# Cross attention to 257 keys: the last key in one product, the heads picked out by VectorE, the row sums split between ScalarE and VectorE

## The chip, the cores and the metric

The kernel runs on one core of a Trainium2 chip. Its time is the device time of the whole program, in microseconds (us). TensorE is PE in the rows (PEld is its weight load), VectorE is DVE, ScalarE is ACT, GpSimd is POOL and SyncE is SP.

## The reference, cut to what matters

The program is a stack of twelve sublayers on x of 128 x 32 tokens with 128 channels. Sublayers 1, 7 and 10 are cross attentions of 16 heads (8 channels each) to a context of 257 keys for each batch row; the change is in these alone. The first reads:

```python
scale = HEAD_DIM ** (-0.5)
q = (xq @ Wq.T).reshape(B, SQ, NUM_HEADS, HEAD_DIM)
kv = (xkv @ Wkv.T).reshape(B, SKV, 2, NUM_HEADS, HEAD_DIM)
k, v = (kv[:, :, 0], kv[:, :, 1])
att = jax.nn.softmax(jnp.einsum('bxhd,byhd->bhxy', q, k) * scale, axis=-1)
x = jnp.einsum('bhxy,byhd->bxhd', att, v).reshape(B, SQ, H)
return x @ Wout.T + bout
```

The tenth also masks keys: `scores = jnp.where(mask == 0, -1e9, scores)`. All data are float32.

## The kernel before

`cross_attention` runs three times, under the names a_cross, e_cross and t_cross (the one with the mask). Each engine has its own program, written by hand; semaphores tie them together, and every engine works strictly in the order in which its program is written. The 128 batch rows are 32 tiles of four (4 x 32 tokens = 128 partitions). A batch row is a step `step(i, n)`; the loop body holds eight steps, so two tiles. A head has 8 channels; four heads make a group of 32 channels (G = 4 groups, J = 4 places in a group).

For batch row n, PE computes the scores of the four groups into PSUM banks 0 to 3 (`scores`, L2071; with a mask another product each, L2076). `scores(n + 1)` waits for all exponentials of n. DVE takes the negative maxima (`maximum`, L2250), ACT the exponentials E (L2214), DVE their sums and reciprocals (L2260, L2262), POOL multiplies E by the reciprocals (`unit`, L2013), PE turns E (L2125, the first half into bank T_BANK, the second into K_BANK), DVE and ACT copy the halves to ET (L2256, L2199), and PE multiplies with the values (`values`, L2135) into O_BANK. The key projection of the next row (L2055) also uses K_BANK and so waits for ACT's copy of ET; ACT then copies the keys (L2193), just ahead of the next exponentials. In a step PE's order is: scores(n), project_keys(n + 1), side(n), project_values(n + 1), both turns of n - 2, values of n - 3. ACT's is: side_out, second half of ET of n - 3, keys of n + 1, exponentials of n, values of n + 1.

257 keys are two blocks of 128 and one key. Once per tile the last key is added apart. Its weights lie in E's last column; PE turns that column for four batch rows and four groups (L2096, 16 rows), ACT copies it (E_last, L2186). Its values come from a product with the context's last columns, four times repeated (L2111, 16 rows), ACT copies them (v_raw, L2189) and POOL spreads them by `last16` (L2017). Four products (L2144, `last_key`, after the values in the third step of the next tile) add them into O_BANK. O_BANK holds for every channel the results of all four heads of its group; only one of four is its own. ACT copies the bank whole (L2207), and the output projection is four products (L2104) with `wo_of`, a weight that is zero but for one head place each. DVE adds the result to X (L2270).

## Time and profile before

| | us |
|---|---|
| median of 3 runs | 4606.94 |
| lowest and highest | 4599.29, 4607.55 |
| profiled execution | 4604.74 |
| its span | 4602.9 |

The span is from the first to the last instruction of the profiled execution. Busy times are those of one engine; several engines are busy at once, and idle time of one that nobody waits for costs nothing. PEclk is the TensorE clock that was granted, as a share of full speed.

### The profile page before, as it was taken

To read this page: it belongs to the slowest core of one execution; us is meant where nothing else is said; L and a number is where in the kernel's file an instruction comes from. 1 tells how busy PE (TensorE), PEld (TensorE's weight loads), DVE (VectorE), ACT (ScalarE), POOL (GpSimd) and SP (SyncE) were. 2 spreads that over 40 slices of the span, in tenths; PEclk is the share of its full clock that TensorE was granted. 3 is DMA by queue.
4 is the path that set the end of the run, shared out by engine and by line. 5 is a ranking of instruction groups with operands and counts; after the bars stand their busy time and mean duration, and the time that the engine had idled before them with its cause. 6 is when DMAs were issued, how large, how long until landed. Compare 5 with 4: busy or idle time off the path is not lost. (4 is left out here: it accounts for less than half of the span.)

```text
span 4602.9 us, 120099 instructions
## 1 busy us (share of the span) xinstructions
PE 3609.7 (78%) x45714; PEld 2581.9 (56%) x45718; DVE 2836.1 (62%) x6649; ACT 2347.0 (51%) x5169; POOL 2397.8 (52%) x2417
## 2 busy tenths in 40 slices
PE   6999959999998288792966999975389998666836
PEld 4777746666665166452644777643267776343424
DVE  6877756666565424674346778735767776743635
ACT  4777635555554043570214777732367775534613
POOL 5666556666664434663344666642246654714623
PEclk9999979999999599895987999975589999877958
DMA  1111010000000122101221111000010111000023
GB/s 59 33 33 33 24 61 9 5 7 10 10 2 2 58 76 65 35 4 64 73 60 32 35 34 33 24 7 6 0 39 31 33 33 51 2 1 5 2 74 88
DMA packets 90228, 143.73 MB, mean 31 GB/s; under 512 B 9984, under 2 KB 66432, under 8 KB 89344
## 3 DMA queue, kind: packets, MB, share of 16 engines
q1 hardware_dynamic: 79616, 117.56, 8.0%
q0 software_dynamic: 10240, 20.99, 1.6%
q8 instruction: 261, 4.28, 0.4%
q14 instruction: 111, 0.91, 0.1%
HBM read 107.44 MB, written 31.06 MB: 30 GB/s over the span
## 5 line engine op out<-in xcount | busy, mean ns | idle before, releaser
L2013 POOL TENSOR_TENSOR t_cross_E<-t_cross_E,t_cross_inverse 128x1028 f32<-128x1028 f32 x128 | 243.4, 1901 | 218.3 <-DVE t_cross_inverse L2262 218.3
L2013 POOL TENSOR_TENSOR e_cross_E<-e_cross_E,e_cross_inverse 128x1028 f32<-128x1028 f32 x128 | 243.4, 1901 | 207.4 <-DVE e_cross_inverse L2262 207.4
L2013 POOL TENSOR_TENSOR a_cross_E<-a_cross_E,a_cross_inverse 128x1028 f32<-128x1028 f32 x128 | 243.4, 1901 | 205.3 <-DVE a_cross_inverse L2262 205.3
L2810 PE MATMUL l_psum<-l_ffn_w,l_hidden 128*128 128x128 f32 x1536 | 218.4, 285 | 32.4 <-POOL l_hidden L2684 30.8
L2250 DVE TENSOR_REDUCE t_cross_negtop<-t_cross_psum 128x2 f32<-128x514 f32 x256 | 165.4, 688 | 119.7 <-PE t_cross_psum L2076 119.7
L2250 DVE TENSOR_REDUCE e_cross_negtop<-e_cross_psum 128x2 f32<-128x514 f32 x256 | 165.4, 688 | 106.9 <-PE e_cross_psum L2071 105.7
L2810 PEld LDWEIGHTS l_psum<-l_ffn_w,l_hidden 128*128 128x128 f32 x1536 | 190.6, 192 | 70.5 <-POOL l_hidden L2684 42.0
L2250 DVE TENSOR_REDUCE a_cross_negtop<-a_cross_psum 128x2 f32<-128x514 f32 x256 | 165.4, 688 | 105.1 <-PE a_cross_psum L2071 103.7
L2803 PE MATMUL l_psum<-l_hT,l_ffn_w 128*128 128x512 f32 x384 | 204.4, 635 | 0.9 <-ACT l_hT L2867 0.9
L2214 ACT ACTIVATE a_cross_E<-a_cross_psum,a_cross_negtop 128x257 f32<-128x257 f32 x512 | 200.5, 481 | 0.6 <-DVE a_cross_negtop L2250 0.6
L2214 ACT ACTIVATE t_cross_E<-t_cross_psum,t_cross_negtop 128x257 f32<-128x257 f32 x512 | 200.5, 481 | 0.7 <-DVE t_cross_negtop L2250 0.7
L2214 ACT ACTIVATE e_cross_E<-e_cross_psum,e_cross_negtop 128x257 f32<-128x257 f32 x512 | 200.5, 481 | 0.6 <-DVE e_cross_negtop L2250 0.6
L2684 POOL TENSOR_TENSOR l_hidden<-l_hidden,l_less 128x512 f32<-128x512 f32 x96 | 120.1, 1274 | 94.7 <-ACT l_hidden L2891 94.7
L2663 POOL TENSOR_SCALAR l_normed<-inner,l_moments,l_rstd 128x128 f32<-128x128 f32 x192 | 159.1, 840 | 15.1 <-POOL l_rstd L2657 15.1
L2964 DVE TENSOR_TENSOR inner<-l_psum,inner 128x512 f32<-128x512 f32 x48 | 33.2, 691 | 213.4 <-PE l_psum L2795 213.4
L2260 DVE TENSOR_REDUCE t_cross_total<-t_cross_E 128x4 f32<-128x1028 f32 x128 | 155.4, 1214 | 0.0
L2260 DVE TENSOR_REDUCE a_cross_total<-a_cross_E 128x4 f32<-128x1028 f32 x128 | 155.3, 1214 | 0.0
L2260 DVE TENSOR_REDUCE e_cross_total<-e_cross_E 128x4 f32<-128x1028 f32 x128 | 155.3, 1213 | 0.0
L2674 POOL TENSOR_TENSOR l_q<-l_q,l_q_stat 128x512 f32<-128x512 f32 x48 | 50.8, 1059 | 185.4 <-DVE l_q_stat L2944 185.4
L2125 PE MATMUL t_cross_psum<-const_sb,t_cross_E 128*128 128x128 f32 x1024 | 135.5, 276 | 2.9 <-POOL t_cross_E L2013 2.9
L2125 PE MATMUL e_cross_psum<-const_sb,e_cross_E 128*128 128x128 f32 x1024 | 134.2, 274 | 2.9 <-POOL e_cross_E L2013 2.9
L2125 PE MATMUL a_cross_psum<-const_sb,a_cross_E 128*128 128x128 f32 x1024 | 133.9, 274 | 2.9 <-POOL a_cross_E L2013 2.9
(747 smaller groups left out, 11209.8 us busy)
## 6 DMA issues: line engine op xcount, KB each, us to landing
a_cross_context<-context SPq DMA_DIRECT2D x32, 522.0 KB, 3.3
e_cross_context<-context SPq DMA_DIRECT2D x32, 522.0 KB, 3.3
t_cross_context<-context SPq DMA_DIRECT2D x32, 522.0 KB, 3.3
u_moe_all_weights<-pack_u_moe SPq DMA_DIRECT2D x1, 5633.0 KB, 16.4
slots<-l_blank SPq DMA_DIRECT2D x6, 832.0 KB, 12.7
a_moe_x_slots<-slots SPq DMA_DIRECT2D x26, 192.0 KB, 2.9
slots<-a_moe_y_slots SPq DMA_DIRECT2D x26, 192.0 KB, 2.1
c_moe_x_slots<-slots SPq DMA_DIRECT2D x26, 192.0 KB, 2.7
```

Source lines behind the costliest of these rows:

```text
L2013: pool.tensor_tensor(E[:, n % N], E[:, n % N], spread(inverse[:, n % 4], SK, 2), ALU.mult).then_inc(s_unit, 1)
L2125: last = pe.transpose(psum[:, (T_BANK, K_BANK)[c], g * P:(g + 1) * P], E[:, n % N, g, c * P:(c + 1) * P], ident)
L2214: act.activation(E[:, n % N, g], psum[:, g, 0:SK], ACT.Exp, bias=negtop[:, n % 2, g:g + 1]).then_inc(s_exp, 1)
L2250: dve.tensor_reduce(negtop[:, n % 2, at], psum[:, at, 0:SK], AX.X, ALU.max, negate=True).then_inc(s_top, 1)
L2260: dve.tensor_reduce(total[:, n % 2], E[:, n % N], AX.X, ALU.add).then_inc(s_sum, 1)
L2663: last = pool.tensor_scalar(Y1[:, t], c.tile(t), moments[:, 0, t, 0:1], rstd[:, 0, 1, t:t + 1], ALU.subtract, ALU.mult)
L2674: pool.tensor_tensor(groups, groups, spread(q_stat[:, 2], DH, 2), ALU.mult).then_inc(s_soft, 1)
L2684: pool.tensor_tensor(hidden[:, f], hidden[:, f], less[:, f - 2], ALU.add).then_inc(s_late, 1)
L2803: pe.matmul(psum[:, U_BANKS[f % 2]], c.ffn(f * P), hT2[:], start=True, stop=True).then_inc(s_up, 1)
L2810: last = pe.matmul(psum[:, D_BANK, t * P:(t + 1) * P], hidden[:, f, t * P:(t + 1) * P], c.ffn((NF + f) * P), start=(f == 0 and t == 0), st ...
L2964: dve.tensor_tensor(c.chunk(), tiles(psum[:, C_BANK]), c.chunk(), ALU.add).then_inc(s_mid, 1)
```

## The change

The last key's four products become one, and the output projection's four become one.

- **Last key.** POOL makes `last_of`: E's last column of four batch rows and four groups, four times over, times a constant that keeps for each place its own 32 partitions. One small product with `fold` (64 rows, 32 columns) gives for each of 64 pairs (batch row, head) the weights of 32 queries; DVE multiplies them by `own_batch` into E_last. The last key's values are computed in 64 rows (the context's last columns now 16 times repeated), and DVE multiplies them by `own_head` into v_last. One product of v_last and E_last gives the last key's part of the output, apart from O_BANK. ACT copies it to aT.
- **Heads picked out.** DVE adds to aT, for each of the four places j, the bank O_BANK times a column that is 1 for the channels whose head is at place j (L2286 of the changed kernel, four times, each waiting for the one before). Two stand ahead of the maxima and two behind them. Then one product with wo.
- **Sums.** Two of four exponentials also write their sum along the row (`accum_out`); DVE sums the other two groups only.

```diff
+    c["own_place"] = (row[:, None] // S == np.arange(4)[None]).astype(float)
+    c["own_batch"] = (row[:, None] // 16 == np.arange(BPT)[None]).astype(float)
+    c["own_head"] = (row[:, None] % 16 == ch[None] // 8).astype(float)
...
+    SUMMED = 2
-    LAST = BPT * G
+    LAST = BPT * G * J
...
-            def last_values(i, t):
-                pool.wait_ge(s_raw, i * 2 + t + 1)
-                pool.tensor_tensor(v_last[:, t % 2], spread(v_raw[:, t % 2], BPT, 1),
-                                   core.const("last16")[0:LAST].rearrange("p (b c) -> p b c", c=P), ALU.mult).then_inc(s_last, 1)
+            def last_weights(i, t):
+                h = t % 2 * BPT
+                pool.wait_ge(s_unit, i * N + 4 * t + 4)
+                if tile_exists(i, t - 2):
+                    pool.wait_ge(s_el, i * 2 + t - 1)
+                pool.tensor_tensor(last_of[:, t % 2], spread(E[:, h:h + BPT, :, MAIN], J, 3),
+                                   spread(spread(core.const("own_place"), G, 1), BPT, 1), ALU.mult).then_inc(s_last_of, 1)
...
                 if n % 4 == 1:
...
-                        pe.transpose(psum[0:LAST, V_BANK, SIDE], E[:, h:h + 4, :, MAIN].rearrange("p n g -> p (n g)"),
-                                     ident).then_inc(s_el, 1)
+                        pe.wait_ge(s_last_of, i * 2 + t)
+                        pe.matmul(psum[0:LAST, V_BANK, 2 * P:2 * P + S], last_of[:, (t - 1) % 2].rearrange("p b g j -> p (b g j)"),
+                                  core.const("fold"), start=True, stop=True).then_inc(s_el, 1)
+                    if tile_exists(i, t - 2):
+                        pe.wait_ge(s_aT, i * 2 + t - 1)
+                        pe.matmul(psum[:, V_BANK, BESIDE], aT[:, t % 2], w("wo"), start=True, stop=True).then_inc(s_out, 1)
                 if n % 4 == 2:
+                    if tile_exists(i, t - 2):
+                        pe.wait_ge(s_done, i * 2 + t - 1)
...
-                        pe.wait_ge(s_O, i * 2 + t - 1)
-                        for j in range(J):
-                            last = pe.matmul(psum[:, V_BANK, SIDE], O[:, t % 2, j].rearrange("p b s -> p (b s)"), wo_of[:, j],
-                                             start=(j == 0), stop=(j == J - 1))
+                        pe.matmul(psum[:, V_BANK, SIDE], v_last[:, (t - 1) % 2], E_last[:].rearrange("p b s -> p (b s)"),
+                                  start=True, stop=True).then_inc(s_alone, 1)
...
                 if n % 4 == 0 and tile_exists(i, n // 4 - 1):
-                    pe.wait_ge(s_O, i * 2 + n // 4)
+                    pe.wait_ge(s_aT, i * 2 + n // 4)
...
-                for b in range(BPT):
-                    last = pe.matmul(psum[:, O_BANK, b * P:(b + 1) * P], v_last[:, t % 2, b], E_last[:, t % 2],
-                                     start=False, stop=(b == BPT - 1))
...
-                    act.activation(E_last[:, (t - 1) % 2], psum[0:LAST, V_BANK, SIDE], ACT.Copy).then_inc(s_E_last, 1)
-                    act.activation(v_raw[:, t % 2], psum[0:LAST, V_BANK, SIDE], ACT.Copy).then_inc(s_raw, 1)
+                if n % 4 == 2 and tile_exists(i, t - 1):
+                    act.wait_ge(s_alone, i * 2 + t)
+                    if tile_exists(i, t - 3):
+                        act.wait_ge(s_out, i * 2 + t - 2)
+                    act.activation(aT[:, (t - 1) % 2], psum[:, V_BANK, SIDE], ACT.Copy).then_inc(s_begun, 1)
...
-                act.activation(O[:, t % 2].rearrange("p j b s -> p b j s"),
-                               psum[:, O_BANK].rearrange("p (b j s) -> p b j s", b=BPT, s=S), ACT.Copy).then_inc(s_O, 1)
...
+                    if g < SUMMED:
+                        act.activation(E[:, n % N, g], psum[:, g, 0:SK], ACT.Exp, bias=negtop[:, n % 2, g:g + 1],
+                                       accum_out=total[:, n % 2, g:g + 1]).then_inc(s_exp, 1)
...
-                dve.tensor_reduce(total[:, n % 2], E[:, n % N], AX.X, ALU.add).then_inc(s_sum, 1)
+                dve.tensor_reduce(total[:, n % 2, SUMMED:], E[:, n % N, SUMMED:], AX.X, ALU.add).then_inc(s_sum, 1)
...
+            def pick(i, t, places):
+                out = aT[:, t % 2].rearrange("p (b s) -> p b s", s=S)
+                for j in places:
+                    if j == 0:
+                        dve.wait_ge(s_begun, i * 2 + t + 1)
+                        dve.wait_ge(s_pv, i * N + 4 * t + 4)
+                    else:
+                        dve.wait_ge(s_picked, (i * 2 + t) * 3 + j)
+                    dve.scalar_tensor_tensor(out=out, in0=psum[:, O_BANK].rearrange("p (b j s) -> p b j s", b=BPT, s=S)[:, :, j],
+                                             scalar=in_group[:, j:j + 1], in1=out, op0=ALU.mult, op1=ALU.add
+                                             ).then_inc(s_aT if j == J - 1 else s_picked, 1)
...
-                              np.repeat(context[:, :, SK - 1].reshape(P, TILES, BPT), 4, axis=2)], axis=2)
+                              np.repeat(context[:, :, SK - 1].reshape(P, TILES, BPT), 16, axis=2)], axis=2)
```

The order of instructions is written by hand. PE's queue in the third step of a tile, from the scores to those of the fourth, stood so before (names are output<-inputs, then output rows x columns; L2055 projects keys, L2059 values, L2125 turns E):

```order
L2071 MATMUL a_cross_psum<-a_cross_kT,a_cross_q_heads 128x257 x4
L2055 MATMUL a_cross_psum<-a_cross_context,a_cross_weights 128x257
L2104 MATMUL a_cross_psum<-a_cross_wo_of,a_cross_O 128x128 x4
L2059 MATMUL a_cross_psum<-a_cross_weights,a_cross_context 128x128 x2
L2125 MATMUL a_cross_psum<-const_sb,a_cross_E 128x128 x4
L2121 REGISTER_ALU
L2125 MATMUL a_cross_psum<-const_sb,a_cross_E 128x128 x4
L2135 MATMUL a_cross_psum<-a_cross_ET,a_cross_v 32x128 x8
L2144 MATMUL a_cross_psum<-a_cross_E_last,a_cross_v_last 128x128 x4
L2068 REGISTER_ALU
L2071 MATMUL a_cross_psum<-a_cross_kT,a_cross_q_heads 128x257 x4
```

and stands so now (L2077 are the scores, L2061 and L2065 the projections, L2131 the turns, L2141 the values):

```order
L2077 MATMUL a_cross_psum<-a_cross_kT,a_cross_q_heads 128x257 x4
L2061 MATMUL a_cross_psum<-a_cross_context,a_cross_weights 128x257
L2111 MATMUL a_cross_psum<-a_cross_E_last,a_cross_v_last 128x128
L2065 MATMUL a_cross_psum<-a_cross_weights,a_cross_context 128x128 x2
L2131 MATMUL a_cross_psum<-const_sb,a_cross_E 128x128 x4
L2127 REGISTER_ALU
L2131 MATMUL a_cross_psum<-const_sb,a_cross_E 128x128 x4
L2141 MATMUL a_cross_psum<-a_cross_ET,a_cross_v 32x128 x8
L2074 REGISTER_ALU
L2077 MATMUL a_cross_psum<-a_cross_kT,a_cross_q_heads 128x257 x4
```

The four products with wo_of have become the one with v_last, and nothing stands between the values and the next scores.

DVE's queue before, in the eighth step (the fourth of the second tile), from the third step's copy of ET on; total is the sum, inverse its reciprocal, negtop the maxima:

```order
L2256 COPY a_cross_ET<-a_cross_psum 128x512
L2250 TENSOR_REDUCE a_cross_negtop<-a_cross_psum 128x2 x2
L2260 TENSOR_REDUCE a_cross_total<-a_cross_E 128x4
L2262 RECIPROCAL a_cross_inverse<-a_cross_total 128x4
L2256 COPY a_cross_ET<-a_cross_psum 128x512
```

and now:

```order
L2247 COPY a_cross_ET<-a_cross_psum 128x512
L2286 SCALAR_TENSOR_TENSOR a_cross_aT<-a_cross_psum,const_sb,a_cross_aT 128x128 x2
L2241 TENSOR_REDUCE a_cross_negtop<-a_cross_psum 128x2 x2
L2286 SCALAR_TENSOR_TENSOR a_cross_aT<-a_cross_psum,const_sb,a_cross_aT 128x128 x2
L2251 TENSOR_REDUCE a_cross_total<-a_cross_E 128x2
L2253 RECIPROCAL a_cross_inverse<-a_cross_total 128x4
L2247 COPY a_cross_ET<-a_cross_psum 128x512
L2274 TENSOR_TENSOR a_cross_v_last<-a_cross_psum,const_sb 64x128
```

Two picks into aT stand ahead of the maxima (negtop), two between them and the sums (total), and the multiplication that makes v_last closes the step.

## Rows read from the trace of the kernel before

**Rows 1.** The page, busy time of each engine over the whole span.
```profile
PE 3609.7 (78%) x45714; PEld 2581.9 (56%) x45718; DVE 2836.1 (62%) x6649; ACT 2347.0 (51%) x5169; POOL 2397.8 (52%) x2417
```

**Rows 2.** Windows: stretch, us; busy PE, PEld, DVE, ACT, POOL; PEclk; DMA share; GB/s.
```profile
303.00:319.32 16.32, 15.51 (x174) 11.59 (x173) 13.04 (x22) 11.89 (x33) 10.07 (x7) 1.00 0.10 33
...
3619.00:3635.65 16.65, 16.00 (x193) 12.16 (x193) 12.97 (x22) 11.88 (x33) 10.00 (x8) 1.00 0.10 32
...
1800.00:1820.00 20.00, 16.83 (x95) 12.21 (x94) 7.22 (x21) 7.06 (x14) 2.92 (x4) 1.00 0.15 40
```

**Rows 3.** Timeline of ACT: start, duration, engine, line, out<-in, count; exponentials at tile starts.
```profile
303.11 1.56 ACT L2214 ACTIVATE a_cross_E<-a_cross_psum,a_cross_negtop 128x257 f32<-128x257 f32 x4
...
314.56 1.57 ACT L2214 ACTIVATE a_cross_E<-a_cross_psum,a_cross_negtop 128x257 f32<-128x257 f32 x4
...
319.49 1.57 ACT L2214 ACTIVATE a_cross_E<-a_cross_psum,a_cross_negtop 128x257 f32<-128x257 f32 x4
...
335.75 1.56 ACT L2214 ACTIVATE a_cross_E<-a_cross_psum,a_cross_negtop 128x257 f32<-128x257 f32 x4
...
3616.93 1.57 ACT L2214 ACTIVATE t_cross_E<-t_cross_psum,t_cross_negtop 128x257 f32<-128x257 f32 x4
...
3650.22 1.56 ACT L2214 ACTIVATE t_cross_E<-t_cross_psum,t_cross_negtop 128x257 f32<-128x257 f32 x4
```

**Rows 4.** Timeline, one ordinary step of a_cross on ACT and PE, and ET's copy later.
```profile
306.92 1.56 ACT L2214 ACTIVATE a_cross_E<-a_cross_psum,a_cross_negtop 128x257 f32<-128x257 f32 x4
...
308.35 0.41 ACT L2203 ACTIVATE a_cross_v<-a_cross_psum 128x256 f32<-128x256 f32 x1
...
308.62 0.40 ACT L2177 ACTIVATE a_cross_qT<-a_cross_psum,a_cross_bq 128x128 f32<-128x128 f32 x1
...
308.87 0.64 ACT L2199 ACTIVATE a_cross_ET<-a_cross_psum 128x512 f32<-128x512 f32 x1
...
309.65 0.67 PE L2055 MATMUL a_cross_psum<-a_cross_context,a_cross_weights 128*128 128x257 f32 x2 [0.38 <-ACT a_cross_ET L2199]
...
310.73 1.57 ACT L2214 ACTIVATE a_cross_E<-a_cross_psum,a_cross_negtop 128x257 f32<-128x257 f32 x4
...
316.39 0.60 ACT L2199 ACTIVATE a_cross_ET<-a_cross_psum 128x512 f32<-128x512 f32 x1
```

**Rows 5.** Timeline of PE in the third and fourth steps of the same tile.
```profile
313.98 1.05 PE L2104 MATMUL a_cross_psum<-a_cross_wo_of,a_cross_O 128*128 128x128 f32 x8
...
314.87 0.61 PE L2059 MATMUL a_cross_psum<-a_cross_weights,a_cross_context 128*128 128x128 f32 x4
...
316.86 1.04 PE L2144 MATMUL a_cross_psum<-a_cross_E_last,a_cross_v_last 16*128 16x128 f32 x7
...
317.64 0.49 PE L2071 MATMUL a_cross_psum<-a_cross_kT,a_cross_q_heads 32*128 32x257 f32 x3
...
318.38 0.70 PE L2055 MATMUL a_cross_psum<-a_cross_context,a_cross_weights 128*128 128x257 f32 x2
...
319.01 0.39 PE L2111 MATMUL a_cross_psum<-a_cross_weights,a_cross_context 128*16 128x128 f32 x2
```

**Rows 6.** Groups by line in a_cross: count, busy us, mean ns, idle time before.
```profile
L2250 DVE TENSOR_REDUCE a_cross_negtop<-a_cross_psum 128x2 f32<-128x514 f32 x256 | 165.4, 688 | 105.1 <-PE a_cross_psum L2071 103.7
L2260 DVE TENSOR_REDUCE a_cross_total<-a_cross_E 128x4 f32<-128x1028 f32 x128 | 155.3, 1214 | 0.0
...
L2022 POOL TENSOR_TENSOR X<-X,a_cross_bo 128x128 f32 x28 | 12.7, 454 | 0.0
...
L2189 ACT ACTIVATE a_cross_v_raw<-a_cross_psum 16x128 f32<-16x128 f32 x32 | 8.0, 250 | 0.0
```

**Rows 7.** Single lines elsewhere: count, duration ns min/median/max, first and last start, form.
```profile
L1516 ACT ACTIVATE a_moe_r<-a_moe_ex x1: 229/229/229, 1578.7 to 1578.7; 128x32 f32<-128x32 f32 x1
...
L1712 DVE SCALAR_TENSOR_TENSOR X<-a_moe_got,a_moe_part,X x64: 342/346/403, 1737.3 to 1860.1; 128x128 f32<-128x128 f32 x64
```

**Rows 8.** Timeline, the first instruction of DVE.
```profile
13.90 0.49 DVE L208 BATCH_NORM_STATS2 a_cross_front_ln_stats<-X 128x6 f32<-128x128 f32 x2 [13.90 <-PEq L3026]
```

More of the change, by code:

```diff
@@ L1960, in cross_attention @@
         s_t0, s_t1, s_ET0, s_ET1, s_pv = sc.sem("t0"), sc.sem("t1"), sc.sem("ET0"), sc.sem("ET1"), sc.sem("pv")
-        s_vl, s_raw, s_last = sc.sem("vl"), sc.sem("raw"), sc.sem("last")
-        s_el, s_E_last, s_whole, s_O = sc.sem("el"), sc.sem("E_last"), sc.sem("whole"), sc.sem("O")
+        s_vl, s_v_last, s_last_of = sc.sem("vl"), sc.sem("v_last"), sc.sem("last_of")
+        s_el, s_E_last, s_alone, s_begun = sc.sem("el"), sc.sem("E_last"), sc.sem("alone"), sc.sem("begun")
+        s_picked, s_aT = sc.sem("picked"), sc.sem("aT")
         s_out, s_base, s_done = sc.sem("out"), sc.sem("base"), sc.sem("done")
@@ L2219, in step @@
                     second_half(i, n - 3)
-                if n % 4 == 3 and tile_exists(i, n // 4 - 1):
-                    whole(i, n // 4 - 1)
                 if exists(i, n + 1):
```

72 lines of the change are left out of this document (36 added, 36 removed).

## The prediction, made before the changed kernel had run

> **What bounds the kernel now.** I read the page first, then the timeline of one tile inside a cross attention, then the groups of costliest instructions. The page says that TensorE (PE) is busy for 78% of the span [rows 1], but that is an average over twelve sublayers, and the change touches only the three cross attentions. There the profile of one tile shows PE busy for 15.51 of 16.32 us at full clock, VectorE (DVE) for 13.04, ScalarE (ACT) for 11.89 and GpSimd (POOL) for 10.07; in t_cross, which adds a mask product, 16.00 of 16.65 [rows 2]. Two consecutive tiles give the periods: from the exponentials at 303.11 to those at 335.75 are two tiles, 16.32 us each; in t_cross (3650.22 - 3616.93) / 2 = 16.65 [rows 3].
>
> A tile is four steps, one for each batch row. The starts of the exponentials are 303.11, 306.92, 310.73, 314.56 and 319.49 [rows 3, 4]: three steps of 3.81 to 3.83 us and one of 4.93. The ordinary step is a ring between ACT and PE, to be read in one step [rows 4]: exponentials from 306.92, copy of the values at 308.35 (+1.43), copy of the queries at 308.62 (+0.27), copy of the turned weights ET at 308.87 (+0.25) that ends at 309.51 (+0.64), key projection on PE at 309.65 (+0.14, it waited for that copy), next exponentials at 310.73 (+1.08: the projection's 0.67, a signal, and the key copy). The sum is 3.81. Without the queries' copy, and with the 0.60 that the ET copy takes elsewhere (316.39), the ring is 3.81 - 0.25 - 0.04 = 3.52. The long step is another thing: ACT's ET copy ended at 316.39 + 0.60 = 316.99, so the key projection could start at 317.13, and it starts at 318.38, 1.25 us later [rows 4, 5]. PE had stood in its own queue: output projection (L2104) 313.98 to the next product at 314.87 is 0.89, and the last key's products (L2144) 316.86 to the scores at 317.64 are 0.78 [rows 5]. So the tile is three rings and one stretch of pure PE queue.
>
> **The change, part by part.** *PE loses* the four products of L2144 (0.78) and three of the four of L2104: 0.89 falls to a quarter, 0.22 [rows 5]. *It gains* one product of the last key (v_last by E_last): 0.22 for a plain one, 0.39 as L2111's row has for a single one with weights of another shape [rows 5]; I take 0.32. It also gains a small product with 64 columns in place of the transposition of 16 (+0.1, half of a plain product, since it moves 32 columns but twice). PE's queue would fall from 16.32 to 16.32 - 0.78 - 0.89 + 0.22 + 0.32 + 0.1 + 0.1 = 15.4; the last 0.1 is an estimate for one more switch of weight shapes, from the excess of 0.32 over 0.22.
>
> *ACT loses* E_last and v_raw (0.25 each [rows 6]) and the copy "whole". Neighbours overlap: the queries' row is 0.40 and the next one starts 0.25 later [rows 4]; with 0.09 to 0.15 of overlap a row of 0.25 costs the ring 0.10 to 0.16. ACT gains the copy that begins aT, 128 x 128 without a pointer: 0.16 too, since a row of 16 x 128 has as many elements to a partition. It stands in the ring of the fourth step.
>
> *The ring then sets the end.* With PE out of the way the tile is four rings, 4 x 3.52, plus queries 0.25 + 0.04, plus aT 0.16: 14.53; I take 14.5. Into every ring the change puts a new term: two of the four exponentials also write their sum (L2205). Call r what one such sum adds to the ring; the tile is then **14.5 + 8 r**. No row of the trace has an accumulator output, so r is bounded by the nearest rows. Lower end: an ACT instruction that overlaps its neighbours costs 0.16 for 128 elements and 0.27 for 256 (308.35 to 308.62), so one element leaves 0.16 - 0.11 = 0.05, say 0.06 [rows 4, 6]. Upper end: the read has to await the end of its exponential, which gives up the overlap (spacing 1.43 / 4 = 0.36, one row 1.56 - 3 x 0.36 = 0.48 [rows 4], so 0.12), and then takes a whole small row, 0.20 to 0.23 after L1516's 229 ns for 32 elements [rows 6, 7]: 0.32 to 0.35. I take the middle, **r = 0.19**: I expect the lost overlap, or a good part of it, and a small instruction that itself overlaps. The tile is then 14.5 + 1.52 = 16.02, against 16.32: -0.30. For t_cross the scores need the mask product too; the same tile plus 0.08 for that, 16.10 against 16.65: -0.55.
> The Trainium skill, "VectorE: DVE Perf Modes", section "Two Vector instructions with no wait between them", says that an operation that also writes out its accumulator is two instructions, the main one and an accumulator read. It says so of VectorE; if ScalarE does likewise, each of the 768 summed exponentials here brings a second instruction, and the rule speaks against the change; no row of this trace can show it.
>
> *DVE* reduces two heads' groups instead of four: 1.21 falls to about 0.69, which L2250 takes for 514 elements [rows 6]. Per tile that is -4 x 0.52 = -2.1. It gains E_last and v_last and four picks of 128 x 128 with a pointer, 0.35 each at most (L1712 [rows 7]), the picks 0.40 apart because each waits for the one before: +2.1. DVE's busy time stays at 13.0, so its load does not matter; its order does. Two picks stand ahead of the maxima of the fourth step, and the next exponentials wait behind them. From the start of the last exponential: 0.36 + values copy 0.26 + aT 0.31 + 0.05 + picks 0.80 + first maximum 0.69 + 0.04 = 2.51. The ring's own way there is 0.36 + 0.26 + 0.16 + 0.60 + 0.14 + 1.08 = 2.60. They are covered by 0.09 us, no more. The last two picks delay sums, reciprocal and POOL's product, but what waits for that (the turn two steps on) comes after the scores of the following step, and the shorter sum gives back 0.52 of the 0.80. The new wait of PE's values on aT is for something 1.5 us old.
>
> *POOL* loses the 512 elements of L2017 and gains a product of 64 elements, between nothing and 0.45 (the row of L2022 has 128 elements and 0.45 [rows 6]). PE now waits for it before the small product of the second step, where it already waited for POOL's unit(); that step has the longest ring, so some 0.3 more is covered.
>
> *Outside the loop.* The constants shrink from 1943 to 1567 columns; with X's 4096 the first instruction that needs them starts at 13.90 [rows 8], so at most 376 / 6039 x 13.9 = -0.9 us; I take 0.8. The context's load grows by 48 of 1044 columns and the transfers are a tenth of the window. PE's busy share falls to about 14.4 / 16.0 = 90%; a stretch with 16.83 of 20 busy was granted full clock [rows 2], so I charge nothing.
>
> **The sum.** The first tiles and the last have no or only part of this; I count 29 of 32. 2 x 29 x 0.30 = 17.4, 29 x 0.55 = 16.0, 0.8 at the start: -34 us. The profiled execution took 4604.7 (span 4602.9), the median is 4606.9; 4604.7 - 34 = 4571, on the median's scale **4573 us**.
>
> **The rivals.** *B, the sums cost more than they free (slower).* The accumulator read waits and blocks, r = 0.28: the tile is 14.5 + 2.24 = 16.74 everywhere, +0.42 in a and e, +0.09 in t: 58 x 0.42 + 29 x 0.09 - 0.8 = +26, 4633. At r = 0.32 it would be 4662. It decides from r = 0.24, where 58 x (8r - 1.82) + 29 x (8r - 2.15) = 0. For it: the ring has no slack of its own; against: small ACT rows do overlap. The skill's rule, taken for ScalarE, is this case with two full small instructions.
> *C, the sums are nearly free.* At r = 0.06 the ring is 15.0, and PE's own queue of 15.4 to 15.6 takes over: -0.8 and -1.0 a tile, 58 x 0.8 + 29 x 1.0 + 0.8 = -76; at r = 0.11 the ring and queue mix, about -56. I put the case at 4542.
> *D, the picks come late.* If the picks are 0.50 apart and not 0.40, the fourth step's exponentials wait 0.11 more and the late reciprocals another 0.15: 0.3 a tile eats the gain, 87 x 0.3 = 26, 4599. For it: the cover is 0.09.
> *E, the stall does not go.* If something else stood behind PE's queue in the long step, that step would stay at 4.93 and the other three would grow by 2 r each: 87 x 1.14 = +99, 4706. Against: the ET copy was done 1.39 us before the projection [rows 4, 5].
>
> **How the numbers follow.** Forecast (r from 0.13 to 0.225) 0.43; C 0.17; D 0.13; B 0.25; E 0.02. Faster by over 0.2% (9 us, about what a measurement of this kernel can tell from no change) is the forecast, C and a third of D: 0.64. Within it is the rest of D and a little of B: 0.11. Slower: 0.25. The range goes from 4545 (near C's point) to 4633 (B's point); beyond them lie some 0.2.
>
> **What would show it.** Right: the period of the exponentials near 16.0 with no long step; the two summed exponentials spaced 0.55 instead of 0.36; no PE wait over 0.4 ahead of the key projection that ACT did not cause. Wrong: the spacing of the summed ones at 0.64 or more (B) or under 0.45 (C); maxima that end after the key copy in the fourth step (D); the long step still there (E).

## The result, and the profile after

| | before | after |
|---|---|---|
| median of 4 runs each, us | 4603.11 | 4529.06 |
| lowest and highest, us | 4597.06, 4607.55 | 4522.06, 4535.61 |
| span of the profiled execution, us | 4602.9 | 4529.1 |

The ratio is 0.984, with a 95% interval from 0.9819 to 0.986: 74 us or 1.6% faster. In a second comparison on another occasion (e0 below) it was 0.987, from 0.9842 to 0.9898, or 60 us; one of the four executions there took 4624.59 us at a lower granted clock (0.824 against 0.891 to 0.894) and is not in that ratio. When the forecast was made the median before was 4606.94, of three executions; with a fourth it is 4603.11. The forecast was 4573, 34 us under the former, with a range from 4545: the direction was right, the gain more than twice as large, and the time outside the range.

Below, "interval" means the time from the first exponential of one step to that of the next; a tile has four. The queries are copied in the **first**, the small product of the last key stands in the **second**, the long one of before and the copy that begins aT are the **third**. Means are over 24 tiles of a_cross, from the starts of the exponentials in the trace.

| interval, us | first | second | third | fourth | tile | tile in t_cross |
|---|---|---|---|---|---|---|
| before | 3.81 | 3.82 | 4.94 | 3.75 | 16.32 | 16.65 |
| after | 4.00 | 4.01 | 3.90 | 3.80 | 15.71 | 15.90 |

The page after, busy time of each engine (against [rows 1]): PE and DVE fell by 75 and 26 us; ACT's rows went from 5169 to 5745.
```profile
PE 3535.1 (78%) x44662; PEld 2466.6 (54%) x44662; DVE 2810.2 (62%) x7222; ACT 2348.1 (52%) x5745; POOL 2329.9 (51%) x2417
```

Windows after, one tile of a_cross and one of t_cross (against [rows 2]; columns as there):
```profile
302.04:317.75 15.71, 15.00 (x164) 10.61 (x164) 12.85 (x28) 12.01 (x40) 9.35 (x7) 1.00 0.11 36
3570.00:3585.90 15.90, 15.40 (x181) 11.06 (x180) 12.79 (x29) 12.03 (x41) 9.34 (x7) 1.00 0.11 35
```
The clock is full in both, as before. PE is still busy for 95% of a tile of a_cross, and yet this says little: the first and the third interval are set by something else, as a table further down shows.

Timeline after, from the end of the first interval to the start of the fourth (against [rows 4, 5]):
```profile
301.32 0.32 POOL L2023 TENSOR_TENSOR a_cross_last_of<-a_cross_E,const_sb 128x64 f32<-128x64 f32 x1 [0.18 <-POOL a_cross_E L2015]
...
301.79 0.27 PE L2101 MATMUL a_cross_psum<-const_sb,a_cross_last_of 128*64 128x32 f32 x2 [0.16 <-POOL a_cross_last_of L2023]
...
302.04 0.47 ACT L2205 ACTIVATE a_cross_E<-a_cross_psum,a_cross_negtop 128x257 f32<-128x257 f32 x1
...
302.40 0.20 ACT L2205 ACTIVATION_READ_ACCUMULATOR a_cross_E<-a_cross_psum,a_cross_negtop 128x1 f32 x1
302.49 0.48 ACT L2205 ACTIVATE a_cross_E<-a_cross_psum,a_cross_negtop 128x257 f32<-128x257 f32 x1
...
302.94 0.85 ACT L2208 ACTIVATE a_cross_E<-a_cross_psum,a_cross_negtop 128x257 f32<-128x257 f32 x2
...
303.92 0.63 ACT L2194 ACTIVATE a_cross_ET<-a_cross_psum 128x512 f32<-128x512 f32 x1
...
304.95 0.70 PE L2061 MATMUL a_cross_psum<-a_cross_context,a_cross_weights 128*128 128x257 f32 x2
...
306.06 0.47 ACT L2205 ACTIVATE a_cross_E<-a_cross_psum,a_cross_negtop 128x257 f32<-128x257 f32 x1
...
308.10 0.64 ACT L2194 ACTIVATE a_cross_ET<-a_cross_psum 128x512 f32<-128x512 f32 x1
...
308.29 0.74 DVE L2286 SCALAR_TENSOR_TENSOR a_cross_aT<-a_cross_psum,const_sb,a_cross_aT 128x128 f32<-128x128 f32 x2 [0.42 <-ACT a_cross_aT L2184]
...
308.88 0.67 PE L2061 MATMUL a_cross_psum<-a_cross_context,a_cross_weights 128*128 128x257 f32 x2
...
308.94 1.28 DVE L2241 TENSOR_REDUCE a_cross_negtop<-a_cross_psum 128x2 f32<-128x514 f32 x2
...
309.96 0.47 ACT L2205 ACTIVATE a_cross_E<-a_cross_psum,a_cross_negtop 128x257 f32<-128x257 f32 x1
```
Three things are to be seen. A sum on ScalarE is a second row, ACTIVATION_READ_ACCUMULATOR, 0.20 us long; it starts 0.36 us after its exponential, where the next exponential would have started, and the next one starts at +0.45 (302.04, 302.49, 302.94). A sum therefore adds **0.09 us**. PE's small product (L2101) waits 0.16 us for POOL's product of 64 elements. And the long interval is gone: 306.06 to 309.96 is 3.90. PE had waited at this place before too, in the second step, for POOL's unit(). Timeline of before:
```profile
310.70 0.27 PE L2096 MATMUL a_cross_psum<-const_sb,a_cross_E 128*16 128x128 f32 x1 [0.38 <-POOL a_cross_E L2013]
```

Over the whole program, from the first instruction that computes with a sublayer's weights to its last, a_cross lost 19.6 us, e_cross 21.4 and t_cross 23.8, together 64.8 of the 73.8 us between the two spans. The other 9 lie in code that the change does not touch: the stretch between e_cross and t_cross took 342.6 us before and 329.8 after, and that between a_cross and e_cross 1884.3 before and 1888.4 after. Windows of before and then of after, the first stretch behind e_cross:
```profile
3000.46:3143.09 142.63, 115.02 (x2966) 67.01 (x2967) 60.57 (x156) 53.95 (x88) 65.54 (x92) 0.79 0.02 7
```
```profile
2963.40:3106.00 142.60, 110.06 (x3332) 66.97 (x3332) 64.68 (x166) 57.35 (x92) 67.80 (x94) 0.87 0.02 7
```
After does more matrix products in the same time (3332 against 2966), at a granted clock of 0.87 against 0.79. In the traces of all kernels below this stretch between the sublayers was either 329 to 332 us, with a clock of 0.85 to 0.88 in its first 142.6 us, or 336 to 343, with 0.79 to 0.83. It did not go with the speed: 340.9 us in the fastest (e7), 342.8 in e11, 328.9 in e0, 329.2 in e13. It may go with the sums: all six kernels with no sum on ScalarE had the long one, and nine of the twelve with some had the short one. With one trace of each kernel what decides it stays open, and so does whether these 13 us belong to the change. The intervals are the better measure of the mechanism.

### The profile page after: what moved, and what is told of

Its sections match the earlier page's. It is cut to its first block and busy times, and to the rows that moved or that the text cites. A ratio compares the mean times of both kernels' runs of the same rounds, so it can differ in the third digit from the quotient of the medians.

```text
span 4529.1 us, 119692 instructions
## 1 busy us (share of the span) xinstructions
PE 3535.1 (78%) x44662; PEld 2466.6 (54%) x44662; DVE 2810.2 (62%) x7222; ACT 2348.1 (52%) x5745; POOL 2329.9 (51%) x2417
## 5 line engine op out<-in xcount | busy, mean ns | idle before, releaser
L2131 PE MATMUL a_cross_psum<-const_sb,a_cross_E 128*128 128x128 f32 x1024 | 134.6, 275 | 2.2 <-POOL a_cross_E L2015 2.1
L2131 PE MATMUL e_cross_psum<-const_sb,e_cross_E 128*128 128x128 f32 x1024 | 134.4, 275 | 2.2 <-POOL e_cross_E L2015 2.1
L2131 PE MATMUL t_cross_psum<-const_sb,t_cross_E 128*128 128x128 f32 x1024 | 134.3, 275 | 2.1 <-POOL t_cross_E L2015 2.1
L2814 PEld LDWEIGHTS l_psum<-l_qT,l_ctx 32*32 32x32 f32 x6144 | 65.7, 107 | 115.8 <-issue 110.1
L2188 ACT ACTIVATE t_cross_kT<-t_cross_psum,t_cross_weights 128x257 f32<-128x257 f32 x128 | 61.0, 477 | 129.1 <-PE t_cross_psum L2061 129.1
L2188 ACT ACTIVATE a_cross_kT<-a_cross_psum,a_cross_weights 128x257 f32<-128x257 f32 x128 | 61.0, 477 | 121.2 <-PE a_cross_psum L2061 121.2
L2188 ACT ACTIVATE e_cross_kT<-e_cross_psum,e_cross_weights 128x257 f32<-128x257 f32 x128 | 61.0, 477 | 120.1 <-PE e_cross_psum L2061 120.1
L2205 ACT ACTIVATE e_cross_E<-e_cross_psum,e_cross_negtop 128x257 f32<-128x257 f32 x256 | 118.6, 473 | 0.9 <-DVE e_cross_negtop L2241 0.9
L2205 ACT ACTIVATE a_cross_E<-a_cross_psum,a_cross_negtop 128x257 f32<-128x257 f32 x256 | 118.6, 473 | 0.9 <-DVE a_cross_negtop L2241 0.9
```

The source lines that it names most:

```text
L2131: last = pe.transpose(psum[:, (T_BANK, K_BANK)[c], g * P:(g + 1) * P], E[:, n % N, g, c * P:(c + 1) * P], ident)
L2188: act.activation(kT[:, n % 2], psum[:, K_BANK, 0:SK], ACT.Identity, bias=w("bk")).then_inc(s_k, 1)
L2205: act.activation(E[:, n % N, g], psum[:, g, 0:SK], ACT.Exp, bias=negtop[:, n % 2, g:g + 1], accum_out=total[:, n % 2, g:g + 1]).then_inc(s ...
L2814: last = pe.matmul(psum[rows, C_BANK, b * S:(b + 1) * S], ctx[rows, b], qT[rows, b * S:(b + 1) * S], start=True, stop=True)
```

## The experiments

All ratios are to the kernel before, run beside it on the same chip; "us" is what they make of some 4595. Intervals as above, from a_cross. e7 leaves out three quarters of two kinds of products, and e14 and e15 take the last key's weights from another tile, so these three do not compute the whole result.

| run | ratio (95%) | us | first | second | third | fourth | tile |
|---|---|---|---|---|---|---|---|
| e0, changed kernel again | 0.987 (0.9842 to 0.9898) | -60 | 4.00 | 4.01 | 3.90 | 3.81 | 15.72 |
| e1, no sum on ACT | 1.0004 (0.9991 to 1.0017) | +2 | 3.94 | 4.82 | 3.78 | 3.82 | 16.36 |
| e3b, one | 0.9914 (0.9888 to 0.9939) | -40 | 3.91 | 4.37 | 3.82 | 3.79 | 15.89 |
| e3, three | 0.988 (0.9859 to 0.9901) | -55 | 4.08 | 3.82 | 3.99 | 3.85 | 15.74 |
| e2, four | 0.9922 (0.9901 to 0.9942) | -36 | 4.17 | 3.91 | 4.08 | 3.90 | 16.06 |
| e4, before + split | 1.0056 (1.0038 to 1.0075) | +26 | 3.99 | 3.83 | 4.93 | 3.82 | 16.57 |
| e7, before, short products | 0.9712 (0.9691 to 0.9732) | -132 | 3.81 | 3.83 | 3.59 | 3.76 | 14.98 |
| e15, e1 without the wait | 0.9807 (0.9779 to 0.9835) | -89 | 3.94 | 3.82 | 3.78 | 3.82 | 15.36 |
| e14, changed, no wait | 0.9819 (0.9796 to 0.9841) | -83 | 3.99 | 3.82 | 3.90 | 3.80 | 15.51 |
| e8, picks behind | 0.9967 (0.9957 to 0.9978) | -15 | 3.99 | 4.02 | 3.90 | 4.18 | 16.09 |
| e9, products behind | 0.9985 (0.9973 to 0.9997) | -7 | 4.00 | 4.52 | 3.91 | 3.81 | 16.22 |
| e10, e9 with one sum | 0.9935 (0.9916 to 0.9953) | -30 | 3.90 | 4.42 | 3.81 | 3.80 | 15.93 |
| e11, e9 with none | 0.9923 (0.9906 to 0.9941) | -35 | 3.93 | 4.33 | 3.78 | 3.83 | 15.87 |
| e12, later | 0.9807 (0.9787 to 0.9827) | -89 | 4.00 | 3.78 | 3.86 | 3.82 | 15.46 |
| e13, later, one sum | 0.9793 (0.9774 to 0.9813) | -95 | 3.90 | 3.78 | 3.82 | 3.80 | 15.30 |
| e16, later, none | 0.9842 (0.9817 to 0.9867) | -73 | 3.97 | 3.78 | 3.92 | 3.97 | 15.64 |

One more reading of the traces tells what sets an interval. On ScalarE the next exponentials stand behind the copy of the keys, this waits for PE's key projection, and that for ScalarE's copy of ET. In the ring of the prediction the key projection starts 0.14 us after the copy of ET ends. Where it starts later, PE was still busy with its own queue or had been held up in it. The time from the end of the copy to the key projection, us, mean of the same 24 tiles (the fourth apart for the two tiles of a loop body):

| run | first | second | third | fourth |
|---|---|---|---|---|
| before | 0.14 | 0.29 | 1.39 | 0.15, 0.29 |
| after | 0.14 | 0.39 | 0.14 | 0.14, 0.25 |
| e14 | 0.14 | 0.21 | 0.14 | 0.14, 0.25 |
| e15 | 0.24 | 0.38 | 0.17 | 0.29, 0.42 |
| e12 | 0.14 | 0.15 | 0.19 | 0.14, 0.26 |
| e13 | 0.14 | 0.26 | 0.29 | 0.20, 0.35 |

So before the change only the first interval was the ring's, and the fourth nearly so in every other tile. Now the first and the third are (308.10 + 0.64 + 0.14 = 308.88 in the timeline above), and the fourth in every other tile, where it is 3.74; in the other it is 3.87. The second is PE's.

**The parts one by one: e7, e4.** e7 is the kernel before with

```
-                        for j in range(J):
+                        for j in range(1):
...
-                for b in range(BPT):
+                for b in range(BPT - 1, BPT):
```


> The kernel before with one product instead of four for the output projection and one instead of four for the last key; everything else stays. It leaves out three quarters of both products, so the outputs are not whole. Q: PE's queue of a tile falls by 3/4 x (0.89 + 0.78) = 1.25 us, the long step of 4.93 goes to about 3.8, the tile to 15.1 to 15.4: 87 x 1.0 = -87 us, 4516 us (4500 to 4535). S: without shorter sums on VectorE the stall only moves and the gain is a third of that or less, above 4570 us.

Measured -132 us, more than either theory: Q had the long interval go to 3.8, and counted fewer tiles. Timeline of e7, the exponentials of one tile and the output projection:
```profile
299.56 1.56 ACT L2214 ACTIVATE a_cross_E<-a_cross_psum,a_cross_negtop 128x257 f32<-128x257 f32 x4
...
303.37 1.56 ACT L2214 ACTIVATE a_cross_E<-a_cross_psum,a_cross_negtop 128x257 f32<-128x257 f32 x4
...
306.63 0.39 PE L2104 MATMUL a_cross_psum<-a_cross_wo_of,a_cross_O 128*128 128x128 f32 x2
...
307.20 1.56 ACT L2214 ACTIVATE a_cross_E<-a_cross_psum,a_cross_negtop 128x257 f32<-128x257 f32 x4
...
310.80 1.56 ACT L2214 ACTIVATE a_cross_E<-a_cross_psum,a_cross_negtop 128x257 f32<-128x257 f32 x4
```
The third interval, 307.20 to 310.80, is 3.60 where it was 4.94; the others are as before. The whole 1.34 us of a tile come from PE's queue in that one interval, and VectorE, with all its sums, is not in the way. So the changed kernel's 0.61 is 1.34 less 0.73 that the rest of the change costs.

e4 is the kernel before with `accum_out` in two exponentials and VectorE's sum over the other two.

> The kernel before with nothing but the split of the sums (two of the four exponentials write theirs, VectorE reduces the other two groups). Q: the ring of three steps grows by 0.18 each, the long step, which PE's queue sets, does not: +0.54 x 87 = +47 us at most, less what earlier reciprocals and POOL products give back; 4615 to 4650 us. S: the split is itself a good part of the gain and this kernel is faster than before, 4560 us or so.

The first interval grew by 0.18, two sums at 0.09. The long one, set by PE's queue, did not; in the second and fourth only 0.01 and 0.07 of the 0.18 came through, so those had not been rings alone, as the table above also says. By itself the split costs 26 us.

**How many sums: e1, e3b, e3, e2, e0.** The changed kernel with
```
-    SUMMED = 2
+    SUMMED = 0
```
and with 1, 3 and 4 (with 4 VectorE's sum is gone).

> The changed kernel with all four sums on VectorE again (SUMMED = 0): the products for the last key, the four picks and the order stay. Theory Q (queue): the gain is PE's queue made shorter, and a sum on ScalarE is only a cost of 0.09 us in the ring, eight of them in a tile. Then this kernel is faster than the changed one until PE's queue of about 15.4 us bounds it: 87 tiles x 0.3 = 26 us, 4503 us. Theory S (sums): the picks filled VectorE, 13.0 us a tile with the split and 15.1 without it, so without the split its sums end late, POOL's product and PE's turns follow late, and the tile goes to 16.2 or more: no better than the kernel before, 4595 to 4640 us. I lean to S here.

> The changed kernel with one sum of four on ScalarE (SUMMED = 1), between the changed kernel and e1. Each tile saves 4 x 0.09 us in the ring, in three of the four steps; VectorE's sum takes 0.26 us longer, so reciprocal, POOL's products and the small product of the second step come later. W: the second step goes from 4.01 to 4.3 us or so and the three others give back 0.27: level with the changed kernel, 65 to 80 us under the kernel before. If the sums on ScalarE were the only thing that counts: 105 us under it; if VectorE's load were: some 40 us.

> The changed kernel with three of four sums on ScalarE. The second step was 4.82, 4.37 and 4.01 us with none, one and two, and 3.91 with all four, where ScalarE's ring must set it; the three others together 11.54, 11.52, 11.70 and 12.15. With three: second step 3.8 to 3.9, the others 11.9: 15.75 a tile, level with the changed kernel, 65 to 75 us under the kernel before. My first sum, 14.5 + 4 r for each sum, would have had 0.36 more a tile: 31 us slower than the changed kernel.

> The changed kernel with all four sums on ScalarE (SUMMED = 4); VectorE makes only the reciprocal, behind the last exponential. Q with 0.09 us a sum: eight more in a tile, +0.72 less the 0.3 of the one step that PE's queue and not the ring sets: +0.4 x 87 = +36 us, 4565 us. A theory of the sums in which VectorE is still the bound would have it faster than the changed kernel: 0.69 us of each step leaves VectorE's way to the reciprocal, 87 x 0.2 or more, below 4510 us. The spacing of all exponentials should be 0.45 us.

> The changed kernel once more, beside the three that follow: 74 us under the kernel before, within 8.

With no sum on ScalarE the whole gain is gone. But it is gone in one interval: the second is 4.82, 4.37, 4.01, 3.82, 3.91 with none, one, two, three and four sums, while the first goes from 3.94 to 4.17 and the third from 3.78 to 4.08. e3b was further from the changed kernel than I expected: the second interval grew by 0.36, and the three others gave back 0.18 and not 0.27, since the fourth hardly follows the sums. Its 40 us are the number that the expectation had for VectorE's load as the cause; e15 below, with the same load as e1 and 89 us gained, rules that out. Three sums are level with two; with three or four the second interval is on the ring (0.14 from the copy to the key projection in both). Timeline of e1, the second interval:
```profile
308.80 1.90 POOL L2015 TENSOR_TENSOR a_cross_E<-a_cross_E,a_cross_inverse 128x1028 f32<-128x1028 f32 x1 [1.42 <-DVE a_cross_inverse L2253]
...
310.79 1.56 ACT L2208 ACTIVATE a_cross_E<-a_cross_psum,a_cross_negtop 128x257 f32<-128x257 f32 x4
310.88 0.32 POOL L2023 TENSOR_TENSOR a_cross_last_of<-a_cross_E,const_sb 128x64 f32<-128x64 f32 x1 [0.18 <-POOL a_cross_E L2015]
...
311.34 0.27 PE L2101 MATMUL a_cross_psum<-const_sb,a_cross_last_of 128*64 128x32 f32 x2 [0.96 <-POOL a_cross_last_of L2023]
...
315.61 1.56 ACT L2208 ACTIVATE a_cross_E<-a_cross_psum,a_cross_negtop 128x257 f32<-128x257 f32 x4
```
PE stands 0.96 us before the small product, for POOL, which waited for VectorE's reciprocal. What e1 lost to the changed kernel is this wait: VectorE's sum is part of a chain sum, reciprocal, POOL's unit(), POOL's last_weights(), PE. The record of L2101's waits says it for all of a_cross, in e1 and then after (us, times; after has the wait in the other tiles too, 0.14 us at 317.42, too short for this view):
```profile
  POOL a_cross_last_of L2023: 31.2, 33
```
```profile
  POOL a_cross_last_of L2023: 2.5, 15
```

**The wait taken away: e15, e14.** In both the small product reads the weights of the tile before, which POOL finished long ago:
```
-                        pe.wait_ge(s_last_of, i * 2 + t)
+                        pe.wait_ge(s_last_of, i * 2 + t - 1)
...
-                        pe.matmul(psum[0:LAST, V_BANK, 2 * P:2 * P + S], last_of[:, (t - 1) % 2].rearrange("p b g j -> p (b g j)"),
+                        pe.matmul(psum[0:LAST, V_BANK, 2 * P:2 * P + S], last_of[:, older % 2].rearrange("p b g j -> p (b g j)"),
```
`older` is t, that is the buffer of tile t - 2. POOL's own wait for s_el moves with it, and the first tile keeps its own weights.

> e1 (the changed kernel, no sum on ScalarE) with one thing taken away: PE's small product reads the last key's weights of the tile before, which POOL finished a tile ago, and so does not wait; the output's share of the last key is that of a wrong tile. Theory W (the wait on POOL is what made e1 slow): the second step falls from 4.82 us to about 3.9, the tile from 16.36 to about 15.4, 84 us under e1 and as much under the kernel before. Theory V (VectorE's load and the order of its sums is the bound): the time stays within 30 us of e1, which was level with the kernel before.

> The changed kernel with its two sums on ScalarE; only PE's small product reads the last key's weights of the tile before and so never waits for POOL; the output's share of the last key is that of a wrong tile. W: the second step falls from 4.01 us by the 0.16 that PE stands there, and by what the other steps' sums delay, to 3.8 or 3.85; the others stay at 4.00, 3.90, 3.80: 15.55 a tile, 13 us under the changed kernel. If the second step stays at 4.0, the length of PE's queue sets it and not the wait.

e15 is e1 with the second interval at 3.82 in place of 4.82 and nothing else moved: 1.00 us a tile, 91 us. In the changed kernel the same wait costs 4.01 - 3.82 = 0.19 us a tile; e14 is 23 us under e0 by the two ratios, 18 by the medians (4512.83 and 4530.6). And without the wait the sums on ScalarE are a loss: 15.51 with two of them, 15.36 with none. The PE rows of e15 in that interval:
```profile
310.80 0.72 PE L2077 MATMUL a_cross_psum<-a_cross_kT,a_cross_q_heads 32*128 32x257 f32 x8
311.44 0.70 PE L2061 MATMUL a_cross_psum<-a_cross_context,a_cross_weights 128*128 128x257 f32 x2
312.07 0.30 PE L2105 MATMUL a_cross_psum<-const_sb,a_cross_last_of 128*64 128x32 f32 x2
312.31 0.49 PE L2109 MATMUL a_cross_psum<-a_cross_weights,a_cross_aT 128*128 128x128 f32 x2
312.63 0.61 PE L2065 MATMUL a_cross_psum<-a_cross_weights,a_cross_context 128*128 128x128 f32 x4
...
314.62 0.71 PE L2077 MATMUL a_cross_psum<-a_cross_kT,a_cross_q_heads 32*128 32x257 f32 x8
```
No row waits; 310.80 to 314.62 is 3.82, the length of PE's own queue in this interval. It is the floor there, above the ring.

**The picks: e8.** All four picks behind the maxima of the fourth step.

> The changed kernel with all four picks behind the maxima of the fourth step, none ahead. My sum had the two picks ahead of the maxima covered by 0.09 us. If they are covered, this changes nothing or loses some us (sums, reciprocal and POOL's product of that step come 0.35 us later): 65 to 76 us under the kernel before. If they were late (rival D), the step of 3.90 us falls to the ring's 3.86 or less by more than 0.1 us, 9 us or more are gained.

The third interval, which the two picks ahead of the maxima could have delayed, stays at 3.90: they were covered. The fourth grew from 3.80 to 4.18, and the whole is 45 us behind e0, which neither expectation had. Timeline of e8:
```profile
315.15 0.47 ACT L2205 ACTIVATE a_cross_E<-a_cross_psum,a_cross_negtop 128x257 f32<-128x257 f32 x1
315.27 1.50 DVE L2286 SCALAR_TENSOR_TENSOR a_cross_aT<-a_cross_psum,const_sb,a_cross_aT 128x128 f32<-128x128 f32 x4
...
316.69 0.68 DVE L2251 TENSOR_REDUCE a_cross_total<-a_cross_E 128x2 f32<-128x514 f32 x1
...
316.92 0.64 PE L2141 MATMUL a_cross_psum<-a_cross_ET,a_cross_v 128*32 128x128 f32 x16 [0.30 <-DVE a_cross_aT L2286]
```
PE's values() of the next tile waits 0.30 for the last pick, which must have left the bank. The cover that counted was this one, behind the maxima, not that ahead of them.

**The two products moved to the end of the second step: e9, e10, e11.**
```
                 if exists(i, n - 3):
                     values(i, n - 3)
+                if n % 4 == 1:
+                    behind(i, n)
```
behind() holds the output projection and the small product, which side() gives up. It waits for s_v first, that is for ScalarE's copy of the values out of the bank to which the two write.

> The changed kernel with the last key's small product (which waits for POOL's product of 64 elements) and the output projection moved from the middle of the second step's PE work to its end, behind the values' products. Theory W (a new wait): the 0.16 us that PE stands before the small product, and the 0.3 us that the two products push the values' projection, the turns and the next key projection back, are 0.3 us of each tile; moved to the end they lie in the shadow of the exponentials and 87 x 0.3 = 26 us go: 98 to 102 us under the kernel before. Theory L (length of PE's queue): the products take the same time wherever they stand, and the time stays 74 us under the kernel before, or loses a little because VectorE gets E_last later, just ahead of the next maxima.

> As e9, but only one of four sums on ScalarE (SUMMED = 1). W: four sums at 0.09 us leave the ring of each tile, 87 x 0.36 = 31 us, and VectorE's sum, 0.26 us longer, is not waited for any more: 120 to 130 us under the kernel before. If VectorE's later sums are still waited for (by POOL's product, then the turns), it is no better than e9.

> As e9, but no sum on ScalarE (SUMMED = 0); against e1, which had these sums and the products in the middle, it tells what the wait for POOL's product was worth. W: in e1 PE stood 0.96 us before the small product in each tile; without it the tile goes from 16.36 to 15.4 or less, 80 us or more under the kernel before. A theory in which VectorE's load of 15.1 us a tile is itself the bound has it gain less than 40 us on e1.

Both theories missed: e9 lost 53 us to e0 in place of winning 26. Timeline of e9:
```profile
311.31 0.41 ACT L2205 ACTIVATE a_cross_v<-a_cross_psum 128x256 f32<-128x256 f32 x1
...
311.84 0.48 PE L2119 MATMUL a_cross_psum<-a_cross_weights,a_cross_aT 128*128 128x128 f32 x2 [0.67 <-ACT a_cross_v L2205]
...
312.59 0.28 DVE L2274 TENSOR_TENSOR a_cross_E_last<-a_cross_psum,const_sb 64x128 f32<-64x128 f32 x1 [1.60 <-PE a_cross_psum L2122]
```
The wait for POOL is gone and one for ScalarE's copy of the values stands in its place, 0.67 us, on PE, ahead of the next scores. I had read in the trace of after that this copy ends before the values' products do (303.65 + 0.41 against 303.73 + 0.64), but took no account of the 0.5 us by which the move itself brings PE forward. e11 against e1 still gains 37 us, under the 80 of W. In e11, with no sums on ScalarE, the new wait is shorter. Timeline of e11:
```profile
306.20 0.48 PE L2119 MATMUL a_cross_psum<-a_cross_weights,a_cross_aT 128*128 128x128 f32 x2 [0.33 <-ACT a_cross_v L2205]
```
It stands for the 0.96 of e1, and the second interval falls from 4.82 to 4.33. Under 40 us was the mark of VectorE's load as the bound; e15 rules that out. e10 lies between: 23 us better than e9, 30 under before and far from the 120 of W.

**Later: e12, e13, e16.** Nothing in a step waits for the last key any more. In side():
```
                 if n % 4 == 1:
...
+                    if tile_exists(i, t - 2):
+                        pe.matmul(psum[:, V_BANK, BESIDE], v_last[:, t % 2], E_last[:].rearrange("p b s -> p (b s)"),
+                                  start=True, stop=True).then_inc(s_alone, 1)
                 if n % 4 == 2:
+                    if tile_exists(i, t - 2):
+                        pe.wait_ge(s_aT, i * 2 + t - 1)
+                        pe.matmul(psum[:, V_BANK, BESIDE], aT[:, t % 2], w("wo"), start=True, stop=True).then_inc(s_out, 1)
+                    if tile_exists(i, t - 1):
+                        pe.wait_ge(s_last_of, i * 2 + t)
...
```
On VectorE the first pick is a tensor_scalar that writes, an addition of the last key's part (L2291) follows in the next second step, and ScalarE's copy that began aT is gone.

> A version of the changed kernel in which nothing waits for the last key: the small product stands one step later (third step), its product with the values one further on (second step of the next tile), in a part of the bank of its own, and VectorE adds it to the finished picks; the first pick writes instead of adding, and ScalarE's copy that began the output's operand is gone. VectorE does one addition of 128 x 128 more, 0.28 us. W: no step waits for POOL's product of 64, each PE queue is under its ring, and the tile is the ring's 3 x 3.70 + 3.99 = 15.1 us and little more, against 15.70: 105 to 125 us under the kernel before. L (length of PE's queue, 15.4 us as I summed it, whatever stands where): 15.5 a tile, 90 us under it. If VectorE's order decides, it is no faster than the changed kernel.

> As e12 with one sum of four on ScalarE. If ring and waits are as I think, each tile saves another 4 x 0.09 us as long as PE's queue and VectorE's 0.26 us longer sums stay covered: 14.9 to 15.1 us, 120 to 140 us under the kernel before. If the sums on VectorE come late again, it is slower than e12.

> e12 with no sum on ScalarE: nothing in a step waits for POOL's product of 64. W with PE's queue as the floor of 15.3 us: level with e13 (15.30), 90 to 97 us under the kernel before, so the division of the sums pays for nothing but the wait. If the late sums on VectorE delay the maxima after the picks, as in e1, it is at 15.4 to 15.5, 80 to 88 us under.

e13, with one sum, is the fastest kernel here that computes everything: 95 us under before, and under both results of the changed kernel, but short of the 120 to 140 that I expected. e12's second interval fell to 3.78 as W said, but the tile is 15.46 and the time 89 us under before, L's numbers. L's mechanism is not what the trace shows: by the table above the first interval, 4.00, and the fourth in every other tile are on the ring, and in the third, 3.86, the exponentials start some 0.05 late, for maxima that stand behind VectorE's picks. e12 changes the order, a copy and an addition at once; which part of its gain each makes is not shown. The window of one tile of e13 and its exponentials:
```profile
302.63:317.86 15.23, 15.16 (x163) 10.64 (x164) 13.70 (x29) 11.41 (x35) 9.35 (x7) 1.00 0.12 37
```
```profile
302.63 0.47 ACT L2199 ACTIVATE a_cross_E<-a_cross_psum,a_cross_negtop 128x257 f32<-128x257 f32 x1
...
306.36 0.47 ACT L2199 ACTIVATE a_cross_E<-a_cross_psum,a_cross_negtop 128x257 f32<-128x257 f32 x1
...
310.25 0.47 ACT L2199 ACTIVATE a_cross_E<-a_cross_psum,a_cross_negtop 128x257 f32<-128x257 f32 x1
```
PE is busy for 15.16 of 15.23 us: here its queue is the bound in all intervals but the first (0.20 to 0.35 in the table above), and it is the 15.4 of the forecast, 0.1 less. With no sum on ScalarE (e16) VectorE comes late instead, in the rows of e16 that end the fourth interval:
```profile
310.52 0.27 DVE L2268 TENSOR_TENSOR a_cross_v_last<-a_cross_psum,const_sb 64x128 f32<-64x128 f32 x1
310.72 1.27 DVE L2235 TENSOR_REDUCE a_cross_negtop<-a_cross_psum 128x2 f32<-128x514 f32 x2
```
```profile
311.43 1.57 ACT L2202 ACTIVATE a_cross_E<-a_cross_psum,a_cross_negtop 128x257 f32<-128x257 f32 x4 [0.18 <-DVE a_cross_negtop L2235]
```
The maxima stand right behind v_last on VectorE, and the exponentials wait for them. e16 is 22 us slower than e13, and at 15.64 a tile and -73 us outside both expectations.

## Why the prediction was wrong

- **The long interval was PE's queue: right.** e7 takes PE's products alone away and gets 4.94 to 3.59. Rival E is out.
- **The price of a sum, r = 0.19: wrong, and this is the step that put the time out of its range.** This is the term r of 14.5 + 8 r. It measured 0.09 us, in the rows after, and again in e4's first interval (+0.18 for two). I had taken it that the read awaits the end of its exponential and so costs the overlap of 0.12. It does not: it starts 0.36 us after the exponential's start, while the exponential's row runs to 0.47, and the next one starts 0.09 later. With 0.09 the formula 14.5 + 8 r gives 15.2, that is 0.8 us a tile under the 16.02 of the forecast, 87 x 0.8 = 70 us. That correction alone would have given 4573 - 70 = 4503, below the 4529 measured: the next error pulls the other way. The Trainium skill, "VectorE: DVE Perf Modes", section "Two Vector instructions with no wait between them", has the accumulator as an instruction of its own; the rows show one on ScalarE as well, but its price is 0.09, not the 0.28 of the rival that leaned on it.
- **A tile as a sum of rings, held against a sum of PE's queue: wrong in kind.** I compared 4 rings with 4 queues over the tile, but each interval takes the longer of the two on its own. With two sums the plain ring is 3.52 + 0.18 = 3.70. The ring sets the first (3.70 + 0.29 = 3.99; measured 4.00) and the third (3.70 + 0.16 = 3.86; 3.90). The second cannot go under PE's queue of 3.82 and has the wait on top; the fourth is 3.74 on the ring in one tile and 3.87 on PE's queue in the next. That makes 15.71 of the 15.2, 0.5 us a tile or 43 us the other way. The fault was there in the reading of before: I took its three short intervals of 3.81 to 3.83 for rings, and only the first was (0.14 from ET's copy to the key projection, against 0.29 in the second, where PE also waits 0.38 for POOL). PE's queue for a whole tile was estimated well: 15.4, against 15.36 in e15, where no key projection starts as early as 0.14 after ET's copy.
- **POOL's product "covered": wrong.** "That step has the longest ring" confused the intervals. The queries' copy lengthens the first; the small product stands behind the key projection, in the second, whose ring is plain. It costs 0.19 us a tile in the changed kernel (e14), and would have cost 1.00 without the split (e15).
- **The split "gives back" nothing but 0.52 of the picks' delay: the size of what hung on it was missed.** Without it the change gains nothing (e1). The split is worth 0.65 us a tile only because it shortens the chain to that wait; on the kernel before it costs 0.25, and with the wait taken away 0.15.
- **VectorE: right on load, half right on order.** The picks are 0.35 each, two in 0.74, and those ahead of the maxima were covered (third interval 3.90 in the changed kernel and in e8). The ones behind have a cover too, PE's values(), which I dismissed as "1.5 us old": with all four there, it costs 0.38 us a tile.
- **The rivals.** C was nearest: its own mark was a spacing under 0.45, and 0.45 was measured; its price of -56 at r = 0.11 to -76 holds the result of -74, and that of -60 in e0. But its mechanism, PE's queue throughout, is true only of the second interval and of the fourth in every other tile, and part of the second is the wait for POOL. That its price fits is in part luck.
- **Small terms.** The start gained nothing in this pair (first row of VectorE at 13.93 against 13.90 [rows 8]), not 0.8; over all the traces it lies between 13.2 and 14.5, so one pair could not show it. 29 tiles were too few: 127 steps between first and last exponential are 31.7 tiles, another 2.7 x 0.65 x 3 = 5 us.

Together: 34 + 70 - 43 + 5 = 66 us, against 64.8 in the three sublayers; the remaining 9 us of this comparison lie in untouched code, 12.8 less behind e_cross and 4.1 more ahead of it.

## What to carry to other kernels

Where two engines hand work round a ring, go step by step and take in each the longest of ring, queue and wait, and only then add up; sums over a whole tile hide that one step is bound by something else. Ask of every new wait in which step it stands and what chain ends in it: in the changed kernel moving half a reduction to another engine was worth nothing for the load it took off and much for the reciprocal that came earlier, while in the order of e13 one sum in four on ScalarE was worth 22 us, by the maxima that came on time (e16). And when a product can be put off by a step or two because nobody needs it yet, look at that first: e12 and e13 gained more that way than the changed kernel did by hurrying the chain before it.

## What the runs showed of the hardware

- An exponential of 128 x 257 on ScalarE that also writes its sum is followed by a row ACTIVATION_READ_ACCUMULATOR of 0.20 us; the next instruction starts 0.09 us later than it would without.
- The stretch of untouched code between e_cross and t_cross took 329 to 332 us in some kernels' traces and 336 to 343 in others', at a granted clock of 0.85 to 0.88 or 0.79 to 0.83 in its first 142.6 us, with no relation to the kernel's speed. What decides it is not shown. A comparison of two whole times can hold 13 us of that.
